# A two-layer transformer kernel on one core: who issues the transfers of rotated queries and keys

## What is computed

```python
xn = _layernorm(x, axis=-1)
x = x + _L0_attn_ref(xn, ...) + _L0_ffn_ref(xn, ...)
xn = _layernorm(x, axis=-1)
x = x + _L1_attn_ref(xn, ...) + _L1_ffn_ref(xn, ...)
```

```python
q = apply_rope(proj(Wq)); k = apply_rope(proj(Wk)); v = proj(Wv)
scores = where(causal, q @ k.T / sqrt(32), -inf)
out = softmax(scores) @ v ; return out @ Wo.T
```

## Time and profile before

| what | value |
|---|---|
| median of 3 runs | 1916.48 us (1915.97 to 1921.6) |
| the profiled execution, its own time | 1917.42 us |
| its span, first to last instruction | 1915.6 us |
| mean granted TensorE clock | 0.985 |
| VectorE busy | 1058.0 us (55%) |
| ScalarE busy | 1089.9 us (57%) |
| GpSimd busy | 720.7 us (38%) |
| TensorE in the chain that ended last | 78% |
| transfers `KS<-pr` and `QS<-pr` | 128 each, 192 KB, all issued by SyncE |

### The profile page before, as it was taken

One profiled execution on the slowest core, in us unless ns is written; L12 is line 12 of the kernel. 1 busy time (PEld: TensorE's weight loads), 2 busy tenths in 40 slices (PEclk: granted clock), 3 DMA queues, 4 the chain that ended last, 5 costly groups with the idle time before them and its releaser, 6 DMA issues.

```text
span 1915.6 us, 24671 instructions
## 1 busy us (share of the span) xinstructions
PE 1814.6 (95%) x8656; PEld 1332.0 (70%) x8656; DVE 1058.0 (55%) x2368; ACT 1089.9 (57%) x2445; POOL 720.7 (38%) x628
## 2 busy tenths in 40 slices
PE   5999999999999999998899989999999999999988
PEld 4777777677777576766487667777777766777655
DVE  5546556373557373737347374655535555555553
ACT  2565747475247574747437566565732575757562
POOL 4234343433333444424233252435343425333321
PEclk9999999999999999999999999999999999999989
DMA  6213131130131221304152030314111313131201
GB/s 225 61 45 94 46 83 45 47 114 28 55 91 45 61 77 39 90 15 124 59 158 77 12 108 31 83 46 127 45 54 47 82 34 84 44 83 40 68 11 44
DMA packets 66314, 130.32 MB, mean 68 GB/s; under 512 B 7696, under 2 KB 8720, under 8 KB 65168
## 3 DMA queue, kind: packets, MB, share of 16 engines
q1 hardware_dynamic: 66192, 128.75, 23.1%
HBM read 73.67 MB, written 4.19 MB: 41 GB/s over the span
## 4 chain that ended last, share of the span: by engine, by line
PE 78%; DVE 10%; ACT 6%; issue 3%; POOL 1%; DMA 1%; SPq 0%; DVEq 0%; ACTq 0%; POOLq 0%
PE D L956 17%; PE G L956 13%; PE U L956 12%; PE OE L956 8%; PE OE L1054 7%; PE SS L1038 6%; PE SS L956 6%; PE OE L1017 3%; PE OE L1038 3%; PE SS L1017 3%; DVE xres L925 2%; DVE OE L883 2%; ACT OE L652 2%; ACT pr L671 1%; DVE SS L883 1%
## 5 line engine op out<-in xcount | busy, mean ns | idle before, releaser
L925 DVE TENSOR_TENSOR xres<-D,xres 128x512 f32<-128x512 f32 x352 | 238.5, 688 | 260.3 <-PE D L956 257.8
L671 ACT ACTIVATE pr<-SS 128x512 f32<-128x512 f32 (+3 forms) x512 | 234.0, 499 | 123.7 <-PE SS L1038 121.9
L763 POOL TENSOR_TENSOR hl<-tt,hh 128x512 fp32r<-128x512 f32 x108 | 139.7, 1294 | 380.6 <-ACT hh L689 380.3
L652 ACT ACTIVATE OE<-OE,mp 128x384 f32<-128x384 f32 (+3 forms) x256 | 203.8, 797 | 100.4 <-DVE mp L883 99.6
L883 DVE CUSTOM_DVE_ANT_0 OE<-OE,mask 128x384 f32<-128x384 f32 (+3 forms) x256 | 220.6, 874 | 65.6 <-PE OE L1017 64.5
L781 POOL TENSOR_SCALAR_AFFINE_SELECT pr<-pr 128x512 f32<-128x512 f32 x128 | 81.2, 637 | 334.0 <-ACT pr L671 334.0
L956 PE MATMUL G<-xh,wgh 128*128 128x512 f32 x432 | 177.5, 411 | 9.7 <-DVE tt L936 8.5
L883 DVE CUSTOM_DVE_ANT_0 SS<-SS,mask 128x128 f32<-128x128 f32 (+3 forms) x256 | 169.8, 676 | 29.0 <-PE SS L1017 28.5
L652 ACT ACTIVATE SS<-SS,mp 128x128 f32<-128x128 f32 (+3 forms) x256 | 162.0, 634 | 34.9 <-DVE mp L883 33.7
L1038 PE MATMUL SS<-QS,KS 98*128 98x512 f32 (+2 forms) x512 | 172.4, 383 | 6.9 <-ACT pr L671 5.7
L956 PE MATMUL D<-wdh,hh 128*128 128x512 f32 x432 | 170.9, 396 | 6.6 <-DVE xres L925 6.1
(11 more groups left out here) (123 smaller groups left out, 3722.1 us busy)
## 6 DMA issues: line engine op xcount, KB each, us to landing
KS<-pr SPq DMA_DIRECT2D x128, 192.0 KB, 3.3
QS<-pr SPq DMA_DIRECT2D x128, 192.0 KB, 3.3
raw<-in_wgate_dram SPq DMA_DIRECT2D x27, 512.0 KB, 3.7
raw<-in_wup_dram SPq DMA_DIRECT2D x27, 512.0 KB, 3.7
raw<-in_wdown_dram SPq DMA_DIRECT2D x27, 512.0 KB, 3.7
raw<-in_wqk_dram SPq DMA_DIRECT2D x16, 512.0 KB, 3.5
trig<-in_wv_dram SPq DMA_DIRECT2D x4, 1024.0 KB, 7.2
trig<-in_rope_dram SPq DMA_DIRECT2D x4, 1024.0 KB, 5.0
```

What stands on the lines that cost most here:

```text
L652: act.activation(s, s, ACT.Exp, bias=mp[:, c, at:at + 1], scale=-1.0, accum_out=se[:, c, at:at + 1]) \
L671: act.activation(weights(i)[:, h, skip:W], SB[(i * HG + h) % 3][:, skip:W], ACT.Exp, scale=-1.0) \
L763: pool.tensor_tensor(hl[:, fc, :], tt[:, (blk * nfc + fc) % 2, :], hh[:, fc, :].bitcast(F32), ALU.subtract) \
L925: dve.tensor_tensor(xres[:, rt, :], d[:, :], xres[:, rt, :], ALU.add).then_inc(sem["v_dfree"], 1)
```

## The change

The step `rotate` leaves SyncE's part of the program and is appended to ScalarE's own part of the same step, behind its two copies. The four transfers, their shapes, their semaphores and their waits are the same. `act.wait_ge` and `act.dma_start` now stand in ScalarE's order, so that what ScalarE does next is behind them.

```diff
@@ block.sync @@
-            def rotate(n, t):
-                qk, c = t % 2, t // 2
-                cols = slice(c * W, (c + 1) * W)
-                sp.wait_ge(sem["g_rl"], n("g_rl", 1))
-                sp.wait_ge(sem["a_rh"], n("a_rh", 2))
-                if qk:
-                    sp.wait_ge(sem["p_v"], n("p_v"))
-                for h in range(HG):
-                    sp.dma_start((QS[0:STACK, c, h, :] if qk else KS[0:STACK, h, cols]).bitcast(F32),
-                                 parts[t][h * DH:(h + 1) * DH, :, :]).then_inc(sem["d_later" if c else f"d_stack{h}"], 16)
-
...
@@ block.scalar, rotate @@
                 act.copy(part[:, again[qk], :], parts[t][:, hi_at[qk], :]).then_inc(sem["a_rh"], 1)
+                c = t // 2
+                act.wait_ge(sem["g_rl"], n("g_rl", 1))
+                act.wait_ge(sem["a_rh"], n("a_rh", 2))
+                if qk:
+                    act.wait_ge(sem["p_v"], n("p_v"))
+                for h in range(HG):
+                    act.dma_start((QS[0:STACK, c, h, :] if qk else KS[0:STACK, h, c * W:(c + 1) * W]).bitcast(F32),
+                                  parts[t][h * DH:(h + 1) * DH, :, :]).then_inc(sem["d_later" if c else f"d_stack{h}"], 16)
```

More of the change, by code:

```diff
@@ L621, in store @@
                 sp.dma_start(out[n.b, rt * P:(rt + 1) * P, :], xres[:, rt, :]).then_inc(sem["d_out"], 16)
-            walk(dict(v_load=v_load, v_weights=v_weights, keep=keep, x_next=x_next, rotate=rotate, flip=flip, load=load_next, store=store))
+            walk(dict(v_load=v_load, v_weights=v_weights, keep=keep, x_next=x_next, flip=flip, load=load_next, store=store))
             sp.wait_ge(sem["d_out"], CREDIT["d_out"] + 16 * RT * B)
```

## The result

The changed kernel takes 2064.77 us (median of 4 runs, 2060.03 to 2069.21) against 1916.22 us (1915.87 to 1921.60): ratio 1.0774, 95% interval 1.0754 to 1.0794, slower by 148.5 us. The forecast was 2036 us, in a range of 1978 to 2085, with a chance of 0.96 for slower. The profiled execution took 2069.21 us with a span of 2067.5 us, so it is 151.8 us above the profiled execution of before. That is the number to be explained by the two traces.

The account below looks back on a forecast made before the run. TensorE, busy 1814.6 of 1915.6 us, follows ScalarE with next to no slack at a turn's start. Later turns 95.5, openings 15.6 and 5.2, slack minus 5.3, clock 8.5: 119.5 us, so 2036 us, range 1978 to 2085.

Parts of the forecast that it names:

- The mechanism: In each rotate, waiting (2.02 us) and four issues (2.57 us) hold ScalarE 4.59 us, delaying the turn's first exponential.
- A: Rival at ScalarE's issues: they cost almost nothing (0.05 us), only the wait for GpSimd stays; 1932 us; chance 0.09.
- case B: Rival at ScalarE's issues: price of a plain load, 0.37 us, a rotate holds 3.50 us; 1981 us; chance 0.07.
- C: Rival at ScalarE's issues: dearer than on SyncE, 1.13 us, a rotate holds 6.54 us; about 2153 us; chance 0.10.
- D: Rival at the start of a turn: transfers land earlier, at most 7.5 us back, 1909 us, or same; chance 0.04.
- One of the signs: In the profile after: TensorE's busy time stays near 1820 us, with a longer span.
- Later turns: Twelve turns, first exponential late: six by 7.6 us, five with a tanh 7.9, one 10.4; sum 95.5 us.
- the slack: Ahead of the fifth score matmul, four turns have 1.9, 1.7, 0.7 and 0.6 us spare; minus 5.3 us in all.
- The last rotates: In the four openings, the third rotate's issues hold the fourth's copies; split 3.9 us late, 15.6 us in all.
- The first rotates: In openings, held casts delay transposes: 2.8 us in the third, 1.2 in second and fourth, none in first; 5.2 us.
- the clock: Half clock behind TensorE's waits: ten more turns at 1.7 us, 17 us, or nothing if ScalarE sets the pace; 8.5 taken.
- No recovery: After the fifth score matmul, ScalarE's lag has no gap to be made up in; TensorE recovers nothing later, 0 us.

Follow-up runs that it names:

- The run with time on ScalarE and no transfer: Against the kernel before: ScalarE waits, then makes ten small copies into an unused tile each rotate, SyncE issues all transfers; 2103.22 us, ratio 1.0973.
- the pair with the second and the fourth rotate: Against the kernel before: ScalarE issues only the second rotate's transfers (1922.50 us), or only the fourth's (2006.82 us), 64 each; SyncE issues the rest.
- the runs with unused matmuls: Changed kernel plus unused matmuls ahead of the fifth score block: 26 or 12 a turn, 2068.07 us; number set for each turn, 2056.90 us.
- the run with the waits alone: Against the kernel before: SyncE still issues, ScalarE only waits behind its copies for GpSimd's subtraction and its own copies; 1935.89 us, ratio 1.0099.
- the run with halves: Against the kernel before: ScalarE issues heads 0 and 1 of each rotate, SyncE heads 2 and 3; 2012.64 us, ratio 1.0493.

## Why the prediction was right, and where its sizes were off

**The mechanism** was right in its main parts. An issue is priced as on SyncE (0.62 against 0.60 us; taken were 0.645 with gaps, and four took 2.56 to 2.59). The wait from the first copy to the first issue is 2.0 us behind a held rotate (171.30 to 173.30), as forecast, and a rotate holds ScalarE 4.61 against 4.59 us. The run with time on ScalarE and no transfer, and the pair with the second and the fourth rotate, show that it is held time ahead of the first exponential, and nothing about the transfers. Cases A, B and C fell with the row of 0.62 us; D would have needed issues that cost nothing. The price of case B was summed wrongly: three rotates of 3.50 us from 164.78 end at 175.28, which is 3.4 us late and not 3.8, so some 4 us less in all. One of the signs did not come: TensorE's busy time was to stay near 1820 us and was 1852.1, as more of its matmuls ran at half clock.

**Later turns** came to 99.7 us against 90.2 with the slack. Six plain turns: 43.0 us, where 6 x 7.6 less 5.3 is 40.3. Five with a tanh: 42.6 us against 39.5. The one with two more ScalarE steps: 14.1 us against 10.4; 1.7 us are a stretch of half clock at 679 us in the weighted sums ahead of it, and its last four issues took 3.70 us instead of 2.57, one of them 1.59:

```profile
716.71 1.26 POOL L771 TENSOR_TENSOR pr<-pr 128x512 fp32r<-128x512 f32 x1
...
718.00 3.70 ACTq L642 DMA_DIRECT2D QS<-pr  x4
721.80 1.04 ACT L689 CAST wqkh<-raw 128x1024 fp32r<-128x1024 f32 x1 [6.72 <-issue]
```

**Openings.** The last rotates: 4.04, 4.05, 4.08 and 4.03 us against 3.9. The first rotates: 1.8, 3.5 and 2.1 us at the transposes against 1.2, 2.8 and 1.2. The rest up to the 11.1 us is clock: 5.1 us in the weighted sums ahead of the third opening and 1.6 us behind its transposes, which the forecast did not have, and less 1.6 us each ahead of the second and the fourth, where the kernel before had a stretch of half clock that did not come again.

**The step that was mis-sized is the clock.** It was 8.5 us by a choice halfway between 17 and nothing, and 23.7 us came between the fifth and the seventeenth block, nearly all of it in turns with half clock there, as the runs with unused matmuls show. Two things in that step were wrong. It counted only the turns that had no half clock before, at 1.7 us each, while the wait now is followed by half clock for longer (0.66 of full over 6.80 us in the row of the second turn, against one stretch of 3.3 us in the earlier trace rows). And it took half off for ScalarE setting the pace, while nearly every turn paid: 1.0 to 2.6 us in 14 of 16; the two others are openings that had half clock there before. Of the 31.7 us between the forecast's sum and the measured one this term makes 15.2, the later turns make 9.5 and the openings' first rotates 5.9. Among waits of 2.4 us and more, longer ones did not cost more: with ScalarE held 5.2 us a rotate the term was 26.4 us, with the fourth rotate alone (TensorE waits 4.42 us in the second turn) 26.5 us. In the run with the waits alone TensorE waited under 1 us in most turns, and the term was 5.2 us. So it went by whether there was such a wait, not by its length.

**No recovery.** The forecast held that TensorE would make up nothing later; between the seventeenth block and the last of the turns the shift changed by -0.1 us. It is a sum: +1.0 us in the fifth turn and -1.6 in the eighth, where a stretch of half clock came or fell away, and under 0.4 in each of the others.

The Trainium skill, "DMA: Bandwidth & Descriptors", section "Issuing engines are not separate DMA queues", says that issuing from several engines only saves the sequencer's time to initiate, usually small against the transfer. The trace agrees as to the size: 0.62 of the 3.2 us from issue to landing, which is no later than before (3.3 us); but this time is the whole effect, since on ScalarE it stands ahead of computing. With both queues issuing at once, the run with halves shows a cost of issuing besides: ScalarE's issues stretch from 0.62 to some 0.8 us. The Trainium skill's 50 ns for dispatch, cited in the prediction for GpSimd's path, is given there as one part of a transfer's fixed cost; what GpSimd's row shows for whole issues is 2.16 us for four.

## What to carry to other kernels

An issue of a transfer holds up the issuing engine's own order (0.62 us on ScalarE, 0.60 on SyncE) and does not show as busy time. Ask what stands behind it in that order, since the same 64 issues cost 5 us ahead of idle time and 90 us ahead of the exponential that TensorE waits for. Where TensorE then waits for several us, add the clock behind the wait, about 1.5 us a wait here, for waits of 2.4 to 13 us alike. An engine with 57% of busy time can be full in the very stretch that counts, and moving work within that stretch gained nothing here.

## What the hardware showed beyond what was expected

- Transfers issued by ScalarE while SyncE issues the same kind stretch for ScalarE alone: two in 1.58 us against SyncE's 1.21. Right behind SyncE's four, ScalarE's four took 3.47 us instead of 2.59, though only the first overlaps an issue of SyncE. The medians from issue to landing were 4.2 and 3.7 us there, against 3.2 in the changed kernel.
- With full clock behind TensorE's wait the stretch to the seventeenth block took at most 1.0 us longer than in the kernel before (16 turns of two runs); with half clock there, 1 to 3 us longer in most turns.
- Four issues from GpSimd took 2.16 us, less than from SyncE (2.58) or ScalarE (2.59), and landed in 3.6 to 3.7 us instead of 3.2 to 3.3.
- Stretches of half clock of some 14 to 20 us come in the weighted sums (L1054 before) without a wait of TensorE of over 1.6 us in the 10 us ahead (longest 1.54 us in the changed kernel, 1.41 in the one before and in the run with the waits alone), and at different places in different kernels.
